# Six gathered blocks fetched row by row from another queue, and a different two-largest routine, in a graph, attention and expert layer

## The reference

```python
xn = layernorm(x)
# graph convolution with residual
h   = xn @ W
deg = segment_sum(edge_weight, dst) + 1.0 ; dinv = rsqrt(deg)
agg = segment_sum((dinv[src] * edge_weight * dinv[dst])[:, None] * h[src], dst)
h   = agg + (dinv * dinv)[:, None] * h + b
h   = relu(0.5 * layernorm_affine(h) + 0.5 * xn)
# linear attention over all nodes, 8 heads
q, k = elu(q) + 1, elu(k) + 1
attn = (q @ (k.T @ v)) / max(q . sum(k), 1e-6) @ Wproj + bproj
x = x + h + attn
# experts
z = layernorm(x)
logits = z @ gate_w + gate_b
vals, idx = top_k(logits, 2) ; w = softmax(vals)
y = z + sum_k w_k * (relu(z @ w1[idx_k] + b1[idx_k]) @ w2[idx_k] + b2[idx_k])
x = x + layernorm_affine(y)
```

## Time and profile before

| | us |
|---|---|
| median of 3 runs | 2158.12 |
| lowest, highest | 2157.35, 2164.04 |
| the profiled execution | 2164.04 |
| its span, first to last instruction | 2162.2 |
| mean granted clock of TensorE | 0.812 of full speed |
| PE busy | 1582.0 (73%) |
| DVE busy | 1099.3 (51%) |
| POOL busy | 1050.6 (49%) |
| ACT busy | 480.4 (22%) |

### The profile page before, as it was taken

How to read it: one execution, slowest core, us unless ns; L and a number is a source line. 1 busy time by engine, 2 the same in 40 slices (tenths; PEclk the granted TensorE clock), 3 DMA queues, 4 the chain that set the end, 5 groups by cost and what they waited for, 6 DMA issues and landing times. The chain is left out here.

```text
span 2162.2 us, 34205 instructions
## 1 busy us (share of the span) xinstructions
PE 1582.0 (73%) x7988; PEld 1256.8 (58%) x7989; DVE 1099.3 (51%) x3965; ACT 480.4 (22%) x1376; POOL 1050.6 (49%) x1099
## 2 busy tenths in 40 slices
PE   8999466665666657766666566767664999999997
PEld 5677355544455445544554445545452899998875
DVE  8998334433344434334443334444347555556558
ACT  3445111111011111110111101111113444443324
POOL 1332565655555445555544455455520454554546
PEclk9999677777777767677777677777787999999998
DMA  6114222222222222222222222222219323225348
GB/s 233 30 30 159 82 87 83 84 71 75 78 71 70 66 66 78 78 78 77 66 68 68 70 78 71 65 77 76 70 36 210 110 71 110 72 92 184 97 124 303
DMA packets 105210, 200.53 MB, mean 93 GB/s; under 512 B 24352, under 2 KB 59808, under 8 KB 105152
## 3 DMA queue, kind: packets, MB, share of 16 engines
q0 software_dynamic: 48240, 131.91, 20.7%
q1 hardware_dynamic: 56624, 67.29, 10.2%
q10 hardware_dynamic: 288, 0.66, 0.1%
HBM read 166.18 MB, written 33.60 MB: 92 GB/s over the span
## 5 line engine op out<-in xcount | busy, mean ns | idle before, releaser
L133 POOL DMA_INDIRECT ring<-table,src x782 | 744.7, 952 | 653.0 <-PE bank L1099 404.3
L1099 PE MATMUL bank<-ring,hots 128*128 x1372 | 336.5, 406 | 11.4 <-issue 11.4
L1099 PEld LDWEIGHTS bank<-ring,hots 128*128 128x128 f32 x1372 | 288.0, 210 | 63.7 <-issue 15.3
L985 DVE SCALAR_TENSOR_TENSOR h<-bank,dinv,vecs 128x256 f32<-128x256 f32 x49 | 23.7, 484 | 499.2 <-remote 482.1
L1037 ACT ACTIVATE xn<-x,half_s,half_r (+1 forms) x48 | 28.8, 601 | 949.5 <-remote 924.0
L1632 PEld LDWEIGHTS bank<-one,w 128*128 128x128 f32 x1696 | 205.1, 192 | 10.2 <-issue 3.7
L1640 PE MATMUL bank<-w,one 128*128 128x256 f32 x848 | 205.0, 384 | 7.3 <-DVE y L1704 4.6
L1632 PE MATMUL bank<-one,w 128*128 128x128 f32 x1696 | 207.5, 275 | 1.5 <-issue 1.0
L1605 ACT ACTIVATE one<-bank,b 128x128 f32<-128x128 f32 x424 | 141.7, 366 | 238.4 <-PE bank L1632 202.2
L1551 POOL DMA_INDIRECT spread<-y,to_x x109 | 108.4, 994 | 172.3 <-issue 96.8
L909 DVE TENSOR_SCALAR hots<-iota_t,edge_l 128x128 f32<-128x128 f32 x686 | 180.5, 350 | 2.0 <-issue 0.3
(11 more groups left out here) (293 smaller groups left out, 2552.4 us busy)
## 6 DMA issues: line engine op xcount, KB each, us to landing
w<-in_w SPq DMA_DIRECT2D x32, 512.0 KB
ring<-table,src POOLq DMA_INDIRECT x782
got<-spread SPq DMA_DIRECT2D x11, 1024.0 KB, 10.5
rows<-xn SPq DMA_DIRECT2D x1, 6272.0 KB, 26.2
out<-xn SPq DMA_DIRECT2D x12, 512.0 KB, 5.6
xt<-in_x_cols SPq DMA_DIRECT2D x11, 512.0 KB, 3.6
table<-xn SPq DMA_DIRECT2D x5, 896.0 KB, 6.3
x<-in_x SPq DMA_DIRECT2D x4, 896.0 KB, 11.2
```

The lines of the kernel that those rows point to most:

```text
L133: return pool.indirect_dma_start(out=m.ring[:, b % RING, :], out_offset=None, in_=a.table, in_offset=bass.IndirectOffsetOnAxis(ap=m.src[:, ...
L1099: last = nc.tensor.matmul(agg, hot[:, k, :], two[:, k, :], start=False, stop=False)
```

## The change

Two things change. First, six of the 782 gathered blocks, `BY_ROWS` = 154, 270, 386, 502, 618 and 734, are no longer gathered by POOL. SP copies their 128 indices to a small DRAM tensor and back to one partition. Then it loads an index into a register, and starts a DMA of that one row of the table to a DRAM tensor `side`, 128 times a block, 4.4 rows (128 / 29) after each step of its relay, over the 29 steps of a group. Eight steps into the next group one DMA moves the block from `side` to its slot of the ring, once `freed` allows it, and the relay waits for it at the block's step. POOL skips the block.

Second, `top_two` is written with reductions: the maximum, a product of the equality mask and a row of descending constants, the maximum of that, and the one-hot row from it; then the chosen entry is pushed down by 3e38 and the same is done again. Each of the nine steps before the last is waited for. It reads the logits from their place among all tiles' logits, so the buffer `fresh_logits` goes.

```diff
+ROWS_EVERY = 116
+BY_ROWS = [ROWS_EVERY * (k + 1) + 38 for k in range(6)]
...
+def top_two(dve, c, m, t, score, pick, rest, both):
+
+    down = m.const[:, C_DOWN:C_DOWN + E]
+    of = tile(m.logits, t, E)
     for k in range(2):
...
+        best, one = tile(m.share, t, 2)[:, k:k + 1], tile(m.one[:, k], t, E)
+        c.add(dve.reduce_max(best, of, axis=AX.X))
+        c.wait()
+        settle(dve, m)
+        c.add(dve.scalar_tensor_tensor(score, of, best, down, ALU.is_equal, ALU.mult))
+        c.wait()
+        settle(dve, m)
+        c.add(dve.reduce_max(pick, score, axis=AX.X))
+        c.wait()
+        settle(dve, m)
+        c.add(dve.tensor_scalar(one, down, pick, None, ALU.is_equal))
+        c.wait()
+        settle(dve, m)
+        if k == 0:
+            c.add(dve.scalar_tensor_tensor(rest, one, -3e38, of, ALU.mult, ALU.add))
+            c.wait()
+            settle(dve, m)
+        of = rest
+    return dve.tensor_tensor(both, tile(m.one[:, 0], t, E), tile(m.one[:, 1], t, E), ALU.add)
...
-        CHAIN_RS, CHAIN_H, CHAIN_X1, CHAIN_TOP = 3, 2, 5, 3
+        CHAIN_RS, CHAIN_H, CHAIN_X1, CHAIN_TOP = 3, 2, 5, 9
...
-            for step in range(FULL // 4):
-                sp.wait_ge(landed[step % 8], (step // 8 + 1) * 64)
+            for k, b in enumerate(BY_ROWS):
+                sp.dma_start(a.row_src[k][:, None], m.src[:, b:b + 1]).then_inc(picked, 16)
+            sp.wait_ge(picked, 16 * len(BY_ROWS))
+            GROUPS = ROWS_EVERY // 4
+            SENT = 8
...
+            def relay(step):
+                sp.wait_ge(landed[step % 8], by_pool(step) * 16)
+                for k, b in enumerate(BY_ROWS):
+                    if b // 4 == step:
+                        sp.wait_ge(side_in, k * 16 + 16)
                 sp.sem_inc(gathered, 2)
+
+            def fetch_row(k, r):
+                row = sp.value_load(row_src[0:1, r:r + 1])
+                row = nc.s_assert_within(row, 0, NP - 1, skip_runtime_bounds_check_because="an index of a row of x")
+                sp.dma_start(a.side[k, r:r + 1], a.table[bass.ds(row, 1)]).then_inc(row_in, 16)
+
+            def send_block(k):
+                b = BY_ROWS[k]
+                sp.wait_ge(freed, (b + 2 - RING) // 2 + CREDIT)
+                sp.dma_start(ring[:, b % RING, :], a.side[k]).then_inc(side_in, 16)
...
+            for k in range(len(BY_ROWS)):
+                sp.dma_start(row_src[:], a.row_src[k:k + 1]).then_inc(picked, 16)
+                sp.wait_ge(picked, 16 * (len(BY_ROWS) + k + 1))
+                if k > 0:
+                    sp.wait_ge(row_in, k * (P * 16))
+                r = 0
+                for step in range(GROUPS):
+                    if k > 0 and step == SENT:
+                        send_block(k - 1)
+                    relay(k * GROUPS + step)
+                    while r < (step + 1) * P // GROUPS:
+                        fetch_row(k, r)
+                        r += 1
...
             for b in range(GATHERED_AHEAD, FULL):
+                if b in BY_ROWS:
+                    continue
...
-                        logits = fresh_logits[:] if routed(t, 5) else tile(m.logits, t - 5, E)
-                        dve.tensor_tensor(logits, gate_ps, m.vecs[:, V_GATEB:V_GATEB + E], ALU.add)
+                        dve.tensor_tensor(tile(m.logits, t - 5, E), gate_ps, m.vecs[:, V_GATEB:V_GATEB + E], ALU.add)
```

More of the change, by code:

```diff
@@ L151, in summed @@
     return here
[L154 to L164, removed]
-    for k in range(2):
[L166 to L170, removed]
+def top_two(dve, c, m, t, score, pick, rest, both):
+    down = m.const[:, C_DOWN:C_DOWN + E]
+    of = tile(m.logits, t, E)
+    for k in range(2):
+        best, one = tile(m.share, t, 2)[:, k:k + 1], tile(m.one[:, k], t, E)
[17 more added lines that the diff above has]
+    return dve.tensor_tensor(both, tile(m.one[:, 0], t, E), tile(m.one[:, 1], t, E), ALU.add)
 def keep_warm(nc, m, bank, n):
@@ L691, in layers @@
         mark = sb("mark", [P, 1])
-        fresh_logits = sb("fresh_logits", [P, E])
-        best = sb("best_l", [P, 8])
-        at = sb("at_l", [P, 8], mybir.dt.uint32)
+        row_src = sb("row_src", [1, P], I32)
+        score = sb("score_l", [P, E])
+        rest = sb("rest_l", [P, E])
+        pick = sb("pick_l", [P, 1])
         moments = m.logits[:].rearrange("p t e -> p (t e)")[:, 0:2 * (D + 1)].rearrange("p (c d) -> p c d", c=DC)
@@ L708, in layers @@
             "chain", "chain_rs", "chain_h", "chain_x1", "chain_top", "both_ok", "turn_ok", "start_ok"))
+        picked, row_in, side_in = map(sem, ("picked", "row_in", "side_in"))
         moments_ok, momtr_ok, momT_ok, ctx_ok, ctxT_ok, attend_mm = map(sem, (
@@ L787, in _, with by_pool @@
                 sp.wait_ge(rg.again, 16 * GATHERED_AHEAD)
-            for step in range(FULL // 4):
-                sp.wait_ge(landed[step % 8], (step // 8 + 1) * 64)
-                sp.sem_inc(gathered, 2)
+            for k, b in enumerate(BY_ROWS):
[3 more added lines that the diff above has]
+            SENT = 8
+            def by_pool(step):
+                return sum(b not in BY_ROWS for s in range(step % 8, step + 1, 8) for b in range(s * 4, s * 4 + 4))
@@ L791, in _ @@
+            sp.wait_ge(row_in, len(BY_ROWS) * P * 16)
+            for step in range(GROUPS * len(BY_ROWS), FULL // 4):
+                if step == GROUPS * len(BY_ROWS) + SENT:
+                    send_block(len(BY_ROWS) - 1)
+                relay(step)
             for k in range(FULL % 4 // 2):
-                sp.wait_ge(landed[FULL % RING // 4], FULL // RING * 64 + 32 * (k + 1))
+                sp.wait_ge(landed[FULL % RING // 4], by_pool(FULL // 4 - 8) * 16 + 32 * (k + 1))
                 sp.sem_inc(gathered, 1)
@@ L979, in turn @@
                 if routed(t, 6):
-                    top_two(dve, Count(dve, chain_top, (t - 6) * CHAIN_TOP, CHAIN_TOP), m, t - 6, fresh_logits, best, at,
+                    top_two(dve, Count(dve, chain_top, (t - 6) * CHAIN_TOP, CHAIN_TOP), m, t - 6, score[:], pick[:], rest[:],
                             m.both[:, n, :]).then_inc(both_ok, 1)
@@ L1942 @@
     a.edges = nc.dram_tensor("edges", (NEP, 3), F32).ap()
+    a.side = nc.dram_tensor("side", (len(BY_ROWS), P, D), F32).ap()
+    a.row_src = nc.dram_tensor("row_src_d", (len(BY_ROWS), P), I32).ap()
     a.rows = nc.dram_tensor("rows", (NP, D + 2), F32).ap()
```

## The result

| | before | changed |
|---|---|---|
| median, us | 2161.08 (4 runs) | 2265.57 (4 runs) |
| lowest to highest, us | 2157.35 to 2168.57 | 2261.67 to 2272.95 |
| ratio, 95% interval | 1 | 1.0487 [1.0455, 1.0519] |

What follows compares the result with a forecast made beforehand. It took POOL's gather bursts plus the pauses until PE frees ring blocks to bound the kernel. Gathers -7.5, DVE stalls +38 and longer `top_two` +1.4 made +31.9 us on the 2158.1 us median: 2190 us, range 2147 to 2236.

Steps and rivals of the forecast that it cites:

- What bounds the kernel: In the layers stage, each turn is POOL's burst of 16 gathers, 20 us, plus a pause until PE frees ring blocks.
- the slow stretch: Part of each POOL burst where engines advance one instruction at a time; 14 us in the turn examined.
- The DVE term: In `top_two`: more DVE records would turn 19 unstalled turns into stalled ones, 2.0 us each, +38 us.
- the two kinds of turns: Turns with stalled or unstalled `top_two` on DVE: median POOL pauses behind them 10.1 and 8.05 us, 2.0 us apart.
- The length of `top_two`: On DVE: 3.4 us for 1.6, hidden in DVE's idle time except at the stage's end, +1.4 us.
- The gather term: In POOL's bursts: six gathers less at 1.25 us each, -7.5 us; -13 us kept as the end.
- SP's rows: On SP: 4.4 rows a step take 3.5 us against POOL's 5.0 us, so SP keeps ahead, 0 us.
- the second rival: SP sets the pace: row fetches on SP make PE wait for `gathered`, +115 us, 2270 us; chance 0.08.
- DMAs that nobody waits for: SP's DMA traffic beside POOL's gathers: no sign that gathers grow, 949 ns in the median, so 0 us.
- The port rule: Two-input DVE instructions can lock out GpSimd on their shared port, costing POOL up to 22 us; taken as zero.

Runs made afterwards that it cites:

- the padding: The kernel before with 17 spare-semaphore increments added in the old `top_two`, ahead of its last instruction: 2089.2 us, 0.991.
- one DMA a block: The changed kernel with one DMA of 128 successive table rows a block in place of 128 row fetches; blocks hold wrong rows: 0.986 of the kernel before.
- group 3: Runs on one chip beside the kernel before (2150 us), all with the new `top_two`: 768 row DMAs unused 1.018, index loads only 0.990, `top_two` alone 0.987.
- group 1: First set of follow-up runs, on one chip beside the kernel before (2108 us); `top_two` alone gave 0.994 there.
- the kernel with fixed addresses: The changed kernel with each row DMA reading a row known at build time, without index load or address computation: 2152.4 us, 1.024.
- the rows alone: The changed kernel with the old `top_two`, six blocks still fetched row by row: 2239.9 us, 1.066 of the kernel before.
- group 2: Second set of follow-up runs, on one chip beside the kernel before (2095 us): changed kernel again 1.079, five blocks 1.026, three blocks 1.020.

## Why the prediction was wrong, point by point

**What bounds the kernel: right.** The turn is POOL's burst plus a pause in which PE catches up, and the slow stretch in a burst holds each engine.

**The DVE term, +38 us: wrong in its mechanism.** The step that failed is "with twice the records it will hardly ever be through before: the 19 unstalled turns become stalled ones, 19 x 2.0". Many did become stalled ones (27 turns of about 5 us or more with the new `top_two` alone, 34 with the padding), and nothing was lost: 0.994 and 0.987 with the first, 0.991 with the second, and no longer pauses behind the stalled turns. The 2.0 us between the two kinds of turns was therefore no price of the stall. I read a symptom as a cause, though I had noted that nobody waits for `both`. What it was a symptom of, perhaps a slow stretch that comes early or lasts long and both stalls DVE and delays PE, is argued and not shown.

**The length of `top_two`, 3.4 us: right.** At the stage's end, where nothing stalls it, it takes from 1696.52 to 1699.61 and 0.17 more, 3.3 us. The first and last of its ten instructions, in DVE's timeline of the changed kernel:

```profile
1696.52 0.14 DVE L162 TENSOR_REDUCE share<-logits 128x1 f32<-128x16 f32 x1
...
1699.61 0.17 DVE L179 TENSOR_TENSOR both<-one 128x16 f32<-128x16 f16 x1
```

**The gather term, -7.5 us: not seen.** With one DMA a block, the six skips gave 0.986 beside 0.987. A gain of 7.5 us is 0.35%, within those intervals; -13 us, 0.6%, lies at their edge.

**SP's rows, 0 us: the step that cost the forecast.** It compared 3.5 us of SP with 5.0 us of POOL a step, both at full speed, and called SP ahead. At full speed that holds: 0.93 us a row, 4.1 us a step. What failed is to count it at full speed alone: SP is slow in the same stretch as the others, and 301 of the 768 rows took 3.03 us in the mean, so a row cost 1.75 us and the 4.4 rows of a step 7.7. In the kernel before a step took 7.1 us with its share of the pauses (1379 us from the first gather to the last, over 195 steps), so SP became the slower of the two. I had this in the second rival and mis-sized it there: 2.1 us a slow row for 3.03, three instructions for four, and 14 us of slow stretch a turn for 911 / 43 = 21 us (all rows over 1.3 us counted). Measured are 911 us for slow rows and 432 for quick ones, 1343 in all. The rival had 574 and 740, 1314 in all, with its price of 1.5 us outside: a total that came near by two errors that cancel. That its 2270 us came near the measured 2266 is luck as well, since it put the whole 115 us on SP's pace and nothing on the DMAs. The point at which the rival decides was set too high by them, 1.3 us a row outside, where 0.93 was enough.

**DMAs that nobody waits for, 0 us: wrong, by 3 points.** I argued from the gathers' duration on POOL, and that did not change (the gathers of the changed kernel, in ns as in the earlier trace rows, minimum, median, maximum):

```profile
L135 POOL DMA_INDIRECT ring<-table,src x776: 940/946/1247, 204.4 to 1671.5; - x194
```

The cost came where I didn't look, in PE's lateness behind the burst, beside a longer wait for ACT.

**The port rule: rightly set to zero.** With three two-input DVE instructions more in 44 turns the gathers stand at 946 ns in the median, and `top_two` alone is not slower. Of what the Trainium skill, "SBUF — State Buffer", section "SBUF: two separate sides", says of the shared port pair, these traces show no effect on such gathers. And no run here shows the record queue of "NOTIFIC — the notification-queue block"; what the slow stretch comes from stays open.

**Do the parts add up?** In the groups' ratios: `top_two` -0.6 to -1.3 points, DMAs +3.1 (1.018 against 0.987, group 3), skips about 0. One check is independent of these: in group 1 the kernel with fixed addresses, which has all three, lies 3.0 points above `top_two` alone (1.024 against 0.994). SP's pace is what is left: +4.2 to the rows alone (1.066, group 1), +5.5 to the changed kernel (1.079, group 2). That the sum then gives the 1.079 back is so by construction.

The two ratios of SP's pace are of one chip, the first with the old `top_two`, the second with the new. The kernel before took 2108 and 2095 us beside them, and they themselves 2240 and 2253; from first row to last SP needed 1338 and 1352 us. On the first chip the change cost 4.9%, and SP's pace fits this too: the changed kernel took 2266 and 2253 us on the two chips, 13 us apart, the kernel before 2161 and 2095, 66 apart, and SP needed 1343 and 1352 us. Where SP sets the pace, a chip on which the bursts go better gains little. This last step is argued from two chips, not tested.

The new `top_two` alone beats the kernel before, by 0.6 and 1.3% in two groups. Why it does, and why the padding does about as well, stays open.

## What to carry to other kernels

Before work is put on an idle queue, count what else that queue relays: a wait that stood first in line is now behind the work, and the queue's time must be counted at the speed it has when the others are slow, not at the speed of a quiet stage. Two kinds of turns in one trace are a correlation; to call a difference between them a price, make the cause happen in many more turns (a padding costs one run), look whether it did, before building a sum on it. And a small DMA that nobody waits for isn't free: vary the number at the same bytes.

## What the runs showed of the hardware that I had not expected

- In the slow stretch of a burst SP's instructions too take about 0.7 us each (median of L817 265 ns, but up to 1408), and a dynamic row DMA of four instructions takes 5.0 us or more from start to start, against 0.96 in a pause.
- 768 DMAs of 1 KB beside the gathers, for which nobody waits, cost 3.1 points (1.018 with a base of 0.987), and 2.2 points more than 192 DMAs with the same bytes (1.022, 1.000), while 768 index loads on the same engine cost nothing that shows (0.990 with the same base).
- 17 increments more a turn on DVE made `top_two` take 5 us or more in 34 of 44 turns, and the kernel no slower (0.991).
- The same kernel differs by 3% between chips (2095 to 2161 us). Between two of its profiled executions, spans 2162.2 and 2100.0 us, 59 of the 62 us lie before PE's last visit with `hots`, at 1613.9 and 1555.1 us:

```profile
L1099 PE MATMUL bank<-ring,hots x1372: 376/379/634, 255.4 to 1613.9; 128*128 x196
```

```profile
L1099 PE MATMUL bank<-ring,hots x1372: 376/379/782, 255.5 to 1555.1; 128*128 x196
```
